# TensorE turns the first chunk ahead of the fifth spread row, two unread products fill its waits, and ScalarE normalises the second chunk, in a two-layer Hyena, attention and expert kernel

## The reference

```python
x = L0_attn_u                                     # (2, 2048, 128)
xn = _layernorm(x, axis=-1)                       # (x - mean) / sqrt(var + 1e-5), per token
# in _L0_attn_ref(xn, ...):
res = u @ w_in.T + b_in                           # 128 -> 384 channels
res = _depthwise_conv3(res.transpose(0, 2, 1), conv_w, conv_b)   # three taps along the tokens
...
logits = jnp.einsum('bsh,he->bse', hidden_states, router_w)      # 8 columns beside the 384
...
x = x + _L0_attn_ref(xn, ...) + _L0_ffn_ref(xn, ...)
xn = _layernorm(x, axis=-1)
x = x + _L1_attn_ref(xn, ...) + _L1_ffn_ref(xn, ...)
```

## Time and profile before

| | |
|---|---|
| median of three executions | 621.71 us |
| lowest, highest | 619.81, 622.02 us |
| the profiled execution's own time | 618.25 us |
| its span | 616.4 us |
| TensorE matmul busy | 557.1 us (90%) |
| VectorE, ScalarE, GpSimd busy | 433.7, 314.3, 297.4 us |
| mean granted TensorE clock | 0.986 |

### The profile page before, as it was taken

One profiled execution on the slowest core, in us unless ns is written; L12 is line 12 of the kernel. 1 busy time (PEld: TensorE's weight loads), 2 busy tenths in 40 slices (PEclk: granted clock), 3 DMA queues, 4 the chain that ended last, 5 costly groups with the idle time before them and its releaser, 6 DMA issues.

```text
span 616.4 us, 10602 instructions
## 1 busy us (share of the span) xinstructions
PE 557.1 (90%) x3218; PEld 463.2 (75%) x3218; DVE 433.7 (70%) x1153; ACT 314.3 (51%) x625; POOL 297.4 (48%) x269
## 2 busy tenths in 40 slices
PE   6999999999989898999999999998889787999970
PEld 3879986576778676788888888876667676788870
DVE  6868998909931596335565998998878895566673
ACT  3560336764423444144456764765675854456550
POOL 4720030005561355147332446887735777577770
PEclk9999999999999999999999999999899999999995
DMA  6460031310040530323323223212322232323626
GB/s 206 155 256 18 2 136 27 77 44 2 1 138 0 178 118 1 94 70 89 88 81 85 56 79 94 86 42 85 92 57 64 61 103 84 88 83 89 228 82 230
DMA packets 48525, 54.94 MB, mean 89 GB/s; under 512 B 7045, under 2 KB 40390, under 8 KB 47415
## 3 DMA queue, kind: packets, MB, share of 16 engines
q1 hardware_dynamic: 43686, 42.99, 22.4%
q0 software_dynamic: 4320, 8.99, 4.2%
q10 hardware_dynamic: 466, 2.31, 1.7%
HBM read 36.22 MB, written 15.94 MB: 85 GB/s over the span
## 4 chain that ended last, share of the span: by engine, by line
PE 29%; DVE 11%; issue 8%; POOL 7%; ACT 7%; DMA 3%; SPq 0%; POOLq 0%; ACTq 0%; DVEq 0%
PE banks L1784 4%; PE banks L1786 3%; PE banks L1785 3%; PE banks L1992 3%; PE banks L2143 3%; PE banks L1906 2%; DMA arena<-result_rows 2%; POOL arena L893 2%; POOL result_rows L878 2%; PE banks L1898 2%; DMA result_rows<-arena 1%; PE banks L2128 1%; POOL expert_rows L863 1%; PE banks L1919 1%; PE banks L1920 1%
## 5 line engine op out<-in xcount | busy, mean ns | idle before, releaser
L878 POOL DMA_INDIRECT result_rows<-arena x71 | 69.1, 973 | 27.9 <-issue 16.6
L827 POOL TENSOR_TENSOR arena<-arena 128x512 f32<-128x512 f32 x32 | 40.8, 1274 | 86.2 <-DVE arena L1468 86.2
L863 POOL DMA_INDIRECT expert_rows<-arena x64 | 63.2, 988 | 30.9 <-issue 15.9
L893 POOL TENSOR_TENSOR arena<-arena 128x512 f32<-128x512 f32 x32 | 42.3, 1321 | 65.0 <-DVE arena L1622 64.9
L1622 DVE TENSOR_TENSOR arena<-banks,arena 128x512 f32<-128x512 f32 x48 | 33.0, 688 | 42.5 <-PE banks L1786 33.5
L1992 PEld LDWEIGHTS banks<-arena 128*128 128x128 f32 x384 | 48.8, 191 | 7.5 <-POOL arena L893 3.5
L1992 PE MATMUL banks<-arena 128*128 128x128 f32 x384 | 51.6, 277 | 2.5 <-POOL arena L893 1.5
L1898 PE MATMUL banks<-arena 128*128 128x512 f32 x96 | 50.5, 608 | 2.4 <-DVE arena L1468 1.1
L1906 PEld LDWEIGHTS banks<-arena 128*128 128x128 f32 x256 | 33.0, 191 | 19.0 <-POOL arena L827 14.4
L1174 ACT ACTIVATE arena<-banks 128x512 f32<-128x512 f32 x48 | 28.8, 599 | 36.2 <-PE banks L1786 31.7
L994 ACT ACTIVATE arena<-banks 128x512 f32<-128x512 f32 x48 | 28.7, 597 | 32.5 <-PE banks L1874 32.5
(11 more groups left out here) (277 smaller groups left out, 1625.0 us busy)
## 6 DMA issues: line engine op xcount, KB each, us to landing
arena<-expert_weights SPq DMA_DIRECT2D x64, 128.0 KB, 3.3
arena<-expert_rows SPq DMA_DIRECT2D x71, 66.0 KB, 1.8
arena<-result_rows SPq DMA_DIRECT2D x8, 512.0 KB, 6.1
arena<-in_x SPq DMA_DIRECT2D x7, 512.0 KB, 7.1
arena<-in_dft_f SPq DMA_DIRECT2D x1, 2048.0 KB, 9.9
normed_hi<-xnt_hi SPq DMA_DIRECT2D x1, 2048.0 KB, 6.3
normed_lo<-xnt_lo SPq DMA_DIRECT2D x1, 2048.0 KB, 10.8
arena<-in_dft_i SPq DMA_DIRECT2D x1, 2048.0 KB, 7.7
```

The lines of the kernel that those rows point to most:

```text
L827: nc.gpsimd.tensor_tensor(out=T1[:, q % 3, :], in0=T1[:, q % 3, :], in1=T2[:, q % 2, :], op=ALU.add).then_inc(y_in, 1)
L863: pool.indirect_dma_start(out=xrows, out_offset=bass.IndirectOffsetOnAxis(ap=SLOT[:, k, t:t + 1], axis=0), in_=XNF[:, t, :], in_offset=Non ...
L878: pool.indirect_dma_start(out=yrows, out_offset=bass.IndirectOffsetOnAxis(ap=DEST[:, i, n:n + 1], axis=0), in_=YB[:, i % YBUFS, n, :], in_ ...
L893: nc.gpsimd.tensor_tensor(out=AM0[slot % 2], in0=AM0[slot % 2], in1=WB0[:, m, :], op=ALU.mult).then_inc(weighted, 1)
```

## The change

On TensorE only four rows are spread at first; then comes a product of the identity with the first chunk of x, 128x512, into bank 6, whose result nobody reads, then the turning of chunk 0, then the same unread product again, then `project(0)`. The fifth row and chunk 1 follow before `project(1)`. Chunk 1 is normalised by ScalarE, after the three taps' high parts, from a `means(0)` that covers the tiles 4 to 7. VectorE does `transposed_lo(0)` right behind the first tap's low part, and then the other two taps, `statistics(2)`, `transposed_lo(1)` and `means(1)`. GpSimd takes the third root (`root(2)`) between L794 and the last two steps of the bias.

```diff
-TURNS_BEFORE = {4: (2,), 5: (3,), 6: (4,), 7: (5,), 8: (6,), 9: (7,)}
+TURNS_BEFORE = {1: (1,), 4: (2,), 5: (3,), 6: (4,), 7: (5,), 8: (6,), 9: (7,)}
-ALL_ON_ACT = 2
+ALL_ON_ACT = 1
...
             link(nc.gpsimd.tensor_tensor(out=bias, in0=bias, in1=CWB[:, 2, :], op=ALU.add))
+            root(2)
             pool.wait_ge(spread_in, 6)
...
-            for n in range(2, len(PIECES)):
+            for n in range(3, len(PIECES)):
                 root(n)
...
             def normalise0(j):
-                act.wait_ge(ln_nmr, j // 2)
+                act.wait_ge(ln_nmr, j // 2 + 1)
...
             taps_hi(2)
+            normalise0(1)
             transposed_hi(1)
...
             def means(q):
                 dve.wait_ge(ln_rstd, q + 2)
-                at = slice(8 * q, 8 * q + 8)
+                at = slice(8 * q + (0 if q else TPC), 8 * q + 8)
...
             normalise0(0)
+            means(0)
             taps_lo(0)
-            normalise0(1)
             transposed_lo(0)
             taps_lo(1)
             taps_lo(2)
+            statistics(2)
             transposed_lo(1)
-            statistics(2)
+            means(1)
...
                         for j in turns:
-                            transposed_lo(j)
+                            if j > 1:
+                                transposed_lo(j)
                 if t == 0:
                     statistics(3)
-                    means(1)
...
-            for n in range(5):
-                mm(PS[(0, 1, 2, 3, 7)[n]][:, 0:OD], ONE_ROW, ROWS[:, n, :], start=True, stop=True)\
-                  .then_inc(spread_mm, 1)
+            def spread_row(n):
+                mm(PS[(0, 1, 2, 3, 7)[n]][:, 0:OD], ONE_ROW, ROWS[:, n, :], start=True, stop=True).then_inc(spread_mm, 1)
+            def keep_clocked():
+                mm(PS[6], IDENT, X[:, 0:TPC, :], start=True, stop=True)
+            for n in range(4):
+                spread_row(n)
             pe.wait_ge(ld_ident, 16)
+            pe.wait_ge(first_x, 16)
+            keep_clocked()
             turn_chunk(0)
-            turn_chunk(1)
+            keep_clocked()
             for t in range(T):
+                if t == 1:
+                    spread_row(4)
                 for j in TURNS_BEFORE.get(t, ()):
                     turn_chunk(j)
                 project(t)
```

## The result

The change makes the kernel slower: 627.86 us (median of 20 executions, 621.30 to 631.67) against 621.44 (20 executions, 617.72 to 626.29); ratio 1.0095, 95% interval 1.0071 to 1.0118. That is outside the range of 620.4 to 625.3, and slower by more than 0.5%, to which the prediction gave 0.10. The profiled execution took 626.66 us, 8.4 more than the profiled one of before.

What follows compares the result with a forecast made beforehand. TensorE was taken as the bound from 28.7 us, its start at 28.77 set by VectorE's chain from tile 0's emptying. That moves +1.5, means(1) saves 0.1: +1.4 us, median 623.1, range 620.4 to 625.3.

Steps and rivals of the forecast that it cites:

- TensorE's start: First 13 us: chunk 0 turned at about 9.8, project(0) at 12.3 to 12.75 instead of 14.27, fast products by 14.
- The other taps' low parts: VectorE's two instructions, 1.01 us alone, meet GpSimd's L794 and end at 13.8, between 13.25 and 13.9.
- The root ahead of the bias: GpSimd's third root delays L796 and L797; tile 0's emptying moves from 18.74 to 20.25, project(6) to about 30.2.
- no earlier: Rival: TensorE's clock rises only at about 18.6 again, the fifth row's copy comes late; +2.5 us, chance 0.10.
- the faster side: Rival: the bias does not hold tile 0's emptying, which follows the statistics at 16.7; -2.1 us, chance 0.06.
- TensorE falls back: Rival: after idling from 25.7 and 28.2, TensorE returns slow for some thirteen products; +3.3 us in all, chance 0.06.
- signs of being wrong: Tile 0 before 18.7, product after chunk 4's turning before 28.8, slow products after 20, or changed stage length behind 40 us.
- The late stage: Behind 40 us: stages were to keep their length, so the early shift carries to the end.
- The reference of the sum: Profiled execution before, 618.25 us, 3.5 below the median of three; +1.4 gives 619.65, the same shift puts the median at 623.1.
- the third rival: TensorE falls back to the slow level after idling ahead of project(6): +3.3 us, median 625.0, chance 0.06.

Runs made afterwards that it cites:

- the kernel with the early row: Changed kernel with fifth spread row beside the other four, no unread product before chunk 0's turning, root behind bias, means(1) behind statistics(3): median 620.55 us, ratio 0.998.
- the delayed one: Kernel before with four unread 128x512 products ahead of project(6), a pure delay: median 625.27 us, ratio 1.0070.
- the filled one: Early-row kernel with chunk 2's low part before means(3), means(1) between statistics(3)'s halves, unread products near 172 and 242 us: median 620.91 us, ratio 0.9975.

## Why the prediction was wrong

*TensorE's start:* chunk 0's turning was put at 9.8 and came at 9.99, the first projection at 12.3 to 12.75 and came at 12.46, the fast level by 14 and came at 13.95. Right.

*The other taps' low parts:* they ended at 14.00; 13.8 was taken, between 13.25 and 13.9. They took 1.68 us against 1.01 before. The delay beside GpSimd's L794 is there, and the Trainium skill's "GPSIMD Engine Reference" (spec table: contention for instructions with two SBUF inputs) agrees. Where they start earlier, beside L793 and L794 both, the same two took 2.59 (in the kernel with the early row) and 2.57 (in the one without unread products).

*The root ahead of the bias:* predicted as the place where the gain is lost, tile 0's emptying at 20.25 and `project(6)` at 30.2; measured 20.42 and 30.34. Right; the runs with the root's place alone show that it delays the bias. The fifth row's copy was put at 16.4 and ended at 17.42, still ahead of the root's end at 18.23, so here it costs nothing, as predicted; without the early root it would be what holds the bias (the estimate above).

*The rivals:* the clock rose early, so "no earlier" is out; the faster side is out by the same row at 20.42. The step that failed is the argument against the third, *TensorE falls back*. The prediction had the idle time right (2 us from 25.7 and 1.7 from 28.2; measured 2.26 and 1.43), and priced it right: +3.3 in all against 3.08 to 3.95. It got 0.06 because of the earlier trace rows, one pause of 2.88 us with no slow product behind it. But slow products came in six profiles of six, and that row was one execution of one pause. The same pause, 2.87 to 3.08 us, stands in all eighteen profiles; in nine of them the eight products behind it take 2.07 or 2.08 us instead of 1.15 or 1.16. The unedited copy of the kernel before is one of the nine:

```profile
522.02 2.07 PE L2143 MATMUL banks<-arena 128*128 x8 [2.87 <-ACT arena L1125]
```

So the row could not carry the argument. Nor does it take two long pauses: 2.27 us alone were enough in the last profile of the changed kernel, and 0.58 and 1.43 us in the one without unread products. Why a pause is followed by slow products in one execution and not in the next stays open. The pattern weighed beside that row, on the Trainium skill's page "TensorE: Matmul & The Clock Gate" (HAM oscillation), was the better guide. There the groups of products wait for transfers, here for ScalarE and VectorE; the trace of the change agrees that the next group starts slow.

Two of the prediction's signs of being wrong came: slow products after 20 us, and a stage behind 40 us that changes its length.

*The late stage* was taken to keep its length, without a row for it: this is the second step that failed. From the landmark to the end the six profiles of the changed kernel take 580.3 to 588.6 us, 586.5 on average; the nine of other kernels without a fall ahead of the landmark (once the level has risen) 579.9 to 587.1, 583.2 on average. Over 32 executions of the changed kernel and 88 of the one before the means are 627.86 and 621.85, 6.0 us apart with a standard error of 0.6 (5.2 without the seven and the three longest), and the mean clocks 0.970 and 0.978. The front accounts for 3.5. The other 1.7 to 2.5 go with falls near 180, 250, 445, 495 and 530 us. Those near 180 and 250 us add 1.7 to 3.0 us each. Four of the six profiles of the changed kernel have both, and a fifth has one of them; the two unedited profiles of the kernel before have neither, but the delayed one and the one with the early row have both. Whether the changed kernel has more of them because of its front, or by chance, these runs do not settle.

*The reference of the sum:* the profiled execution of before had only one fall, near 440 us, and the prediction bridged its 3.5 us below the median with a constant. No step depends on it, but it hid that this kernel's executions differ by such falls. The range also ended at 625.3, only 0.3 above the third rival's 625.0, although it allowed a median of three about 1 us of its own; 627.86 lies outside either way.

No version here is shown to beat the kernel before. The three with the early row and the root behind the bias beat the changed one clearly; the filled one is nearest to a gain, 0.9975 (0.9942 to 1.0007).

## What to carry to other kernels

Before making one engine earlier, look for what the earliest consumer waits for on the others: moving a root in front of two steps that nothing had delayed cost 4.0 and 3.0 us at the first consumer where it was moved alone. And when a change lets TensorE run ahead of a chain that it does not shorten, the time won becomes idle time, and idle time ahead of a wait can cost the clock on top. One execution in which a pause passed without a fall does not rule that out: look at the same pause in several executions before giving it a small chance, or fill it.

## What the runs showed of the hardware

- The granted clock in the windows reads 1.00 while the first products run at half rate (0.32 us for 384 columns), yet shows each later fall (0.72 over 30 to 36 us). The durations show both.
- Spread rows, products of one partition, kept TensorE busy for 6.7 us before and the level did not rise; it rose at 13.95 with full 128x512 products from 8.12 on.
- One pause of 2.87 to 3.08 us, the same in eighteen profiles of different versions, was followed by products at half rate in nine of them and at full rate in the other nine.
- Near 172 us pauses of 0.89, 0.96 and 0.69 us within 5 us, with products between, are followed by slow products in some executions and not in others. Each such fall lengthened its stage by 1.7 to 3.0 us; with the pauses filled none came in three profiles, but the mean time was not lower for it.
